# Rotary embedding of a fused attention and FFN kernel: the unturned first pair, and the rotation added in place in the feature tile

## The reference, cut to what matters

```python
def _rope(x, theta):
    T = x.shape[2]
    freqs = theta / 220.0 * _freqs_base()       # 8 frequencies, the first is 0
    ang = jnp.arange(T, dtype=jnp.float32)[:, None] * freqs
    cos, sin = (jnp.cos(ang), jnp.sin(ang))
    xr = x.reshape(*x.shape[:-1], HD // 2, 2)
    a, b = (xr[..., 0], xr[..., 1])
    rot = jnp.stack([a * cos - b * sin, a * sin + b * cos], axis=-1)
    return rot.reshape(x.shape).astype(x.dtype)
...
q = _rope(q, theta)
k = _rope(k, theta)
qk = jnp.einsum('bhkd,bhqd->bhkq', q, k) * scale
attn = _taylor_softmax(qk)          # (1 + x + x*x/2) / its sum
```

## Time and profile before

| | |
|---|---|
| median of 3 runs | 638.67 us (637.12 to 638.91) |
| the profiled execution, its own time | 640.14 us |
| its span, first to last instruction | 638.3 us |
| granted TensorE clock, mean over the span | 0.985 |
| busy: PE, DVE, ACT, POOL | 610.6, 585.2, 534.3, 445.5 us |

### The profile page before, as it was taken

The page is one execution under the profiler, slowest core; times in us unless marked ns, Lnnn a source line. Parts: engine busy times, 40 slices in busy tenths (PEclk is TensorE's granted clock), DMA queues, the critical chain, the costliest instruction groups (busy, mean ns, idle before and its releaser), DMA issues. The chain is left out here.

```text
span 638.3 us, 22975 instructions
## 1 busy us (share of the span) xinstructions
PE 610.6 (96%) x7592; PEld 472.3 (74%) x7592; DVE 585.2 (92%) x1489; ACT 534.3 (84%) x1504; POOL 445.5 (70%) x785
## 2 busy tenths in 40 slices
PE   8899999999999999999999999999999999999975
PEld 7776767676877778777787777678777776878764
DVE  5999999899999999999999989989989999986894
ACT  4267888898898989889898988889888988999972
POOL 2565456777777878787678967777886868764563
PEclk9999999999999999999999999999999999999985
DMA  7101131313232323322233142223232222130211
GB/s 249 34 3 41 24 75 26 76 33 110 45 104 53 97 70 78 89 71 72 51 76 86 46 126 66 69 51 114 52 105 56 76 54 79 30 85 20 68 36 42
DMA packets 55955, 43.67 MB, mean 68 GB/s; under 512 B 7200, under 2 KB 55712, under 8 KB 55840
## 3 DMA queue, kind: packets, MB, share of 16 engines
q1 hardware_dynamic: 55024, 41.42, 24.5%
q10 hardware_dynamic: 816, 0.79, 0.4%
HBM read 18.65 MB, written 8.39 MB: 42 GB/s over the span
## 5 line engine op out<-in xcount | busy, mean ns | idle before, releaser
L1200 ACT ACTIVATE feat<-ps_f 128x512 f32<-128x512 f32 x256 | 147.8, 604 | 9.1 <-PE ps_f L869 7.6
L688 DVE TENSOR_TENSOR kf<-kf 128x896 f32<-128x896 f32 (+1 forms) x128 | 128.8, 1012 | 1.0
L869 PE MATMUL ps_f<-qT,selr 128*128 128x512 f32 x320 | 120.8, 428 | 2.2 <-ACT feat L1200 1.4
L1042 PE MATMUL ps_mt<-kf,vp 128*32 128x153 f32 x2048 | 79.8, 296 | 2.0 <-ACT rm L1229 0.9
L1042 PEld LDWEIGHTS ps_mt<-kf,vp 128*32 128x32 f32 x2048 | 60.1, 109 | 17.9 <-issue 13.8
L1786 POOL TENSOR_TENSOR kf<-kf 128x128 f32<-128x128 f32 x64 | 42.9, 670 | 35.6 <-DVE kf L1550 35.4
L869 PEld LDWEIGHTS ps_f<-qT,selr 128*128 128x128 f32 x320 | 55.2, 189 | 12.3 <-ACT feat L1200 5.3
L688 POOL TENSOR_TENSOR kf<-kf 128x224 f32<-128x224 f32 x64 | 60.1, 939 | 2.2 <-DVE kf L1557 1.9
L1799 POOL TENSOR_TENSOR ve_y<-var_y,epst 128x1 f32<-128x1 f32 x64 | 24.9, 389 | 49.7 <-ACT squares_y L1312 49.2
L1774 POOL TENSOR_TENSOR qsp<-kf,qsp 128x256 fp32r<-128x256 f32 x64 | 54.5, 851 | 2.9 <-ACT qsp L1301 2.9
L1793 POOL TENSOR_TENSOR attT_l<-att,attT_h 128x256 fp32r<-128x256 f32 x56 | 43.4, 776 | 16.0 <-ACT attT_h L1241 15.6
(11 more groups left out here) (205 smaller groups left out, 1994.1 us busy)
## 6 DMA issues: line engine op xcount, KB each, us to landing
xc<-L_attn_x SPq DMA_DIRECT2D x16, 512.0 KB, 4.1
result<-fin SPq DMA_DIRECT2D x64, 128.0 KB, 3.0
xa<-L_attn_x SPq DMA_DIRECT2D x15, 512.0 KB, 3.9
heads_out<-osb SPq DMA_DIRECT2D x224, 32.0 KB, 2.0
shares<-sums SPq DMA_DIRECT2D x112, 64.0 KB
sums<-osb SPq DMA_DIRECT2D x224, 2.0 KB
wkqv<-L_attn_w_kv ACTq DMA_DIRECT2D x2, 256.0 KB, 4.4
xa<-L_attn_x SPq DMA_DIRECT2D x1, 384.0 KB, 5.7
```

What stands on the lines that cost most here:

```text
L688: return eng.tensor_tensor(dims(row, F_MAIN, [[FW, heads], [HD, NR - 1], [1, HD]]), dims(row, F_LIN, [[FW, heads], [0, NR - 1], [1, HD]]), ...
L869: pe.matmul(ps_f[i % 2][:, :], selr[:, i], queries, start=True, stop=True).then_inc(sel_done, 1)
L1042: mm = pe.matmul(ps_mt[qd // 2][VW * h:VW * (h + 1), (qd % 2) * NF:(qd % 2 + 1) * NF], vp[:, s2, qd * HQ + h], kf[:, s2, qd * HQ + h, 0:NF ...
L1200: act.activation(feat[:, p2, i], ps_f[i % 2][:, :], ACT.Square).then_inc(squared, 1)
```

## The change

Three things change together.

1. The rotation leaves the first pair of each head alone: `rope_sin` computes 14 of 16 features of each of the 32 heads (16 of the queries, 16 of the keys), 448 columns where it had 512, into the new tile `turned`; the sources start two words further.
2. `rope_cos` writes all 512 columns straight into the key and query fields of `kf`, and `rope_add` adds `turned` to 448 of them there, in place. With that the waits for the free buffer (`qlo_ready` and `sums_done` of the tile two before) move from `rope_add` to `rope_cos`; `rope_cos` no longer waits for the addition of the tile before. The tiles `t1` and `t2` are gone.
3. `ORDER` is another plan for all five queues, of the same lengths, and `IDLE` has 16 entries where it had 15.

```diff
+            def rotated(t, first):
+                return dims(kf[:, t.two, 0, 0:1], F_LIN + first, [[F_Q - F_LIN, 2], [FW, H], [1, HD - first]])
+
             def rope_cos(t):
-                cos = dims(cosT[:], t.tile * HD, [[0, 2 * H], [1, HD]])
+                cos = dims(cosT[:], t.tile * HD, [[0, 2], [0, H], [1, HD]])
                 if t.n == 1:
                     dve.wait_ge(tables_done, 1)
-                wait(dve, rope_ready, t.n - 1)
+                wait(dve, qlo_ready, t.n - 2)
+                wait(dve, sums_done, t.n - 2)
                 dve.wait_ge(qk_done, t.n)
-                dve.tensor_tensor(t1[:].rearrange("p (h d) -> p h d", d=HD), ps_qk[:, :].rearrange("p (h d) -> p h d", d=HD),
-                                  cos, ALU.mult).then_inc(qk_read, 1)
+                dve.tensor_tensor(rotated(t, 0), ps_qk[:, :].rearrange("p (a h d) -> p a h d", a=2, d=HD), cos, ALU.mult).then_inc(qk_read, 1)
 
             def rope_sin(t):
-                sin = dims(sinT[:], t.tile * HD, [[0, 2 * H], [2, 8], [1, 2]])
+                sin = dims(sinT[:], t.tile * HD + 2, [[0, 2 * H], [2, NR - 1], [1, 2]])
                 if t.n == 1:
                     dve.wait_ge(tables_done, 1)
                 wait(dve, rope_ready, t.n - 1)
                 dve.wait_ge(qk_done, t.n)
-                dve.tensor_tensor(dims(t2[:], 0, [[HD, 2 * H], [2, 8], [1, 2]]), dims(ps_qk[:, :], 1, [[HD, 2 * H], [2, 8], [-1, 2]]),
-                                  sin, ALU.mult).then_inc(qk_read, 1)
+                dve.tensor_tensor(dims(turned[:], 0, [[HD - 2, 2 * H], [2, NR - 1], [1, 2]]),
+                                  dims(ps_qk[:, :], 3, [[HD, 2 * H], [2, NR - 1], [-1, 2]]), sin, ALU.mult).then_inc(qk_read, 1)
 
             def rope_add(t):
                 dve.wait_ge(qk_read, 2 * t.n)
-                wait(dve, qlo_ready, t.n - 2)
-                wait(dve, sums_done, t.n - 2)
-                dve.tensor_tensor(dims(kf[:, t.two, 0, 0:1], F_LIN, [[F_Q - F_LIN, 2], [FW, H], [1, HD]]),
-                                  t1[:].rearrange("p (a h d) -> p a h d", a=2, d=HD),
-                                  t2[:].rearrange("p (a h d) -> p a h d", a=2, d=HD), ALU.add).then_inc(rope_ready, 1)
+                dve.tensor_tensor(rotated(t, 2), rotated(t, 2), turned[:], ALU.add).then_inc(rope_ready, 1)
...
-IDLE = {"fill": (1, 1, 1, 1, 1, 1, 4, 7, 10, 11, 14, 14, 14, 18, 23,), "drain": ()}
+IDLE = {"fill": (1, 1, 1, 1, 1, 1, 4, 7, 9, 9, 9, 9, 13, 18, 20, 28,), "drain": ()}
```

More of the change, by code:

```diff
@@ L180 @@
-        "sum_bias": ((3,), (), ()),
-        "sum_wo": ((4,), (), ()),
+        "centre_bias": ((102,), (), ()),
+        "copy_ffn_weight": ((94,), (), ()),
+        "copy_main": ((33, 83, 141, 209, 278,), (-2,), (494, 562, 636, 707, 779, 853, 921, 990, 1060,)),
+        "copy_q": ((23, 29, 38, 49, 59, 62, 71, 84, 101, 113, 125, 143, 162, 181, 200, 215, 231, 246, 263, 281, 300,
+            317, 334, 352, 372, 387, 405, 423, 440, 457, 476, 493, 512, 528, 547, 566, 582, 600, 617, 635, 654, 670,
+            687, 705, 723, 741, 758, 777, 795, 812, 829, 848, 867, 884, 901, 919, 935, 953, 971, 988, 1006, 1023, 1039,
+            1054,), (), ()),
@@ new lines @@
+        "high_kq": ((5,), (), ()),
+        "high_q": ((14, 17, 24, 30, 42, 50, 60, 67, 78, 91, 103, 114, 126, 145, 163, 183, 201, 217, 233, 251, 268, 288,
+            305, 323, 339, 359, 377, 394, 411, 433, 448, 465, 481, 503, 517, 534, 552, 575, 588, 607, 626, 646, 660,
+            680, 695, 715, 735, 749, 768, 794, 804, 820, 837, 859, 874, 890, 906, 927, 945, 961, 981, 1001, 1020,
+            1036,), (), ()),
+        "high_v": ((9,), (), ()),
+        "sines": ((4,), (), ()),
+        "split_ffn_weight": ((98,), (), ()),
@@ new lines @@
+        "low_ffn_weight": ((137,), (), ()),
+        "low_h": ((14, 18, 27, 39, 54, 65, 78, 86, 98, 106, 121, 136, 145, 156, 169, 198, 220, 240, 268, 286, 304, 324,
+            347, 368, 389, 407, 432, 455, 473, 491, 515, 535, 559, 580, 599, 621, 641, 661, 682, 706, 724, 744, 764,
+            789, 808, 829, 850, 872, 897, 915, 938, 958, 979, 1000, 1023, 1044, 1067, 1086, 1106, 1129, 1152, 1168,
+            1189, 1206,), (), ()),
+        "low_kq": ((6,), (), ()),
+        "low_v": ((15,), (), ()),
@@ new lines @@
+        "normalise_x": ((9, 13, 17, 29, 38, 52, 59, 70, 82, 90, 103, 119, 123, 143, 152, 164, 191, 204, 230, 254, 270,
[11 rows of a table added]
+        "rest_terms": ((64, 112, 175, 251, 330,), (-12,), (586, 666, 751, 837, 925, 1011, 1093, 1186, 1260,)),
+        "rope_add": ((22, 30, 40, 49, 62, 80, 88, 97, 108, 124, 140, 149, 158, 176, 199, 209, 237, 260, 278, 299, 321,
+            342, 364, 384, 404, 427, 452, 469, 488, 512, 536, 553, 578, 598, 617, 640, 659, 683, 703, 725, 745, 769,
+            788, 811, 830, 853, 878, 894, 916, 940, 959, 980, 1001, 1025, 1045, 1066, 1085, 1108, 1130, 1150, 1167,
+            1195, 1212, 1227,), (), ()),
@@ new lines @@
+        "rope_cos": ((20, 25, 35, 47, 61, 79, 87, 96, 107, 122, 139, 148, 157, 172, 197, 208, 236, 258, 275, 293, 315,
+            336, 361, 379, 399, 422, 451, 462, 482, 509, 534, 547, 570, 594, 613, 632, 656, 680, 696, 720, 741, 763,
+            782, 807, 827, 851, 873, 890, 912, 935, 956, 978, 997, 1021, 1043, 1064, 1083, 1105, 1127, 1146, 1162, 1183,
+            1205, 1223,), (), ()),
+        "rope_sin": ((21, 28, 36, 46, 60, 77, 85, 95, 102, 120, 138, 147, 153, 165, 186, 207, 232, 256, 272, 292, 312,
+            333, 357, 374, 395, 417, 450, 461, 480, 502, 533, 545, 568, 589, 605, 631, 651, 670, 691, 713, 734, 755,
+            774, 797, 819, 841, 868, 880, 902, 926, 954, 967, 988, 1014, 1041, 1056, 1077, 1101, 1119, 1141, 1159, 1180,
+            1207, 1217,), (), ()),
```

413 lines of the change are left out of this document (194 added, 219 removed), and 108 rows, old and new, of the table ORDER.

## The result

| | before | after |
|---|---|---|
| median of the runs | 638.33 us (637.12 to 638.91, 4 runs) | 642.93 us (641.67 to 643.64, 4 runs) |
| ratio to before, 95% interval | | 1.0069 (1.0050 to 1.0087) |
| span of the profiled execution | 638.3 us | 641.8 us |

The account below looks back on a forecast made before the run. DVE was taken to set the pace in its fullest stretches, together with PE; 7.8 us saved x 0.62 = 4.8 us off the profiled 640.14 gives 635.3, the median 1.5 us lower, so 634 us, range 629.5 to 641.5.

Parts of the forecast that it names:

- The price of each instruction: DVE rotation: sine 616 ns, addition 613 (650 at most), cosine's new output 0 to 4 ns; 0.132 us saved a tile.
- The dear in-place addition: Rival, DVE addition: stays at 679 ns because of odd words, only the sine saves, 636.3 us; chance 0.09.
- The moved waits: DVE cosine waiting for sums: 1.65 and 4.5 us at tiles 12 and 14 in the old order, 0 in the new.
- The slower rival: The moved wait stalls DVE at the cosine of 8 tiles, giving 642.1 us; chance 0.15.
- the profile had to show above 5 for it: Sign before the cosine: idle released by PE under 1 us in total; above 5 us the slower rival is right.
- How much of it reaches the end: Middle: six full DVE stretches give all, seven others three tenths, so 0.62 of 7.8 us, 4.8 us.
- The prediction's own sign in the profile: DVE idle in the middle: about 30 us confirms 0.62, 27 with a shorter middle all arriving, 35 PE bound.
- PE is the bound: Rival, middle: the saving only lengthens DVE's idle time; 638.7 us, with the order's noise 637 to 640.5; chance 0.20.
- The new order and the idle products: All queues' place tables and two more idle PE matmuls in the fill: 0, with 3 us each way.
- My closing line: Likeliest error: the order, as a gap in fill or drain differing by some us, all DVE durations as forecast.

Follow-up runs that it names:

- new_512: The changed kernel (new order, in-place addition, moved waits) with all 512 columns again in sine and addition: 644.45 us, ratio 1.0097 to the kernel before.
- order_only: The kernel before (old rotation, old waits) with the new ORDER and IDLE: 645.41 us, ratio 1.0123.
- columns_only: The kernel before, old order, waits and tiles, with only sine and addition cut to 448 of 512 columns: 637.19 us, ratio 0.9990.
- half_columns: The kernel before, old order and waits, with sine and addition cut to 256 of 512 columns: 634.58 us, ratio 0.9930.
- mended: The changed rotation in the old order, with the cosine of tiles 12, 14 and 62 moved right ahead of its addition: 638.44 us, ratio 1.0007.
- lean_mended: mended with PE's waits left out where an earlier PE wait already implies them: 636.97 us, ratio 0.9974.
- lean_before: The kernel before with PE's waits left out where an earlier PE wait already implies them: 636.33 us, ratio 0.9972.
- dve_plus: The kernel before with one more DVE product of 128 columns ahead of the cosine in each tile: 646.22 us, ratio 1.0129.

## Why the prediction was wrong

**The price of each instruction**: right. 616 and 613 ns were forecast, 614 and 618 measured, the cosine's new output 1 ns. The dear in-place addition (rival, 0.09) did not come. The Trainium skill, page "Vector Engine (DVE) Microarchitecture Reference", paragraph on the SBUF access granule (it stands in the section on measured stream behaviour), would make pairs at odd words, on both sources, dearer by a quarter. The addition, where only the key half of `kf` begins at an odd word, shows no sign of that. In the new order it takes 692 ns in place (new_512) and 693 ns from contiguous tiles (order_only), both with 512 columns; with 448 columns it takes 618 ns in the kernel after and, from contiguous tiles in the old order, 612 ns in columns_only.

**The moved waits**: right. In the old order they stall DVE by 1.69 and 4.45 us (1.65 and 4.5 forecast) and, at a tile that I had not looked at, by 3.21; the new order avoids them. The slower rival (0.15) named this as the way to a loss, so its time of 642.1 is near the result by another mechanism: the idle time before the cosine is 0.7 us after, and the profile had to show above 5 for it.

**"How much of it reaches the end", 0.62**: the first step that failed. By columns_only it is 0.6 / 7.8 = 0.08, by half_columns 0.15, and in the new order 1.8 / 7.8 = 0.23. The first and the last can't be told from nothing, but neither interval reaches the 4.8 us of the forecast. The step read a stretch with DVE at 98% as one in which DVE sets the pace and gives all. A saving there gives something only if what comes next on DVE is ready sooner too, and DVE's idle time of 31.6 for 26.9 us in columns_only says that mostly it was not. The prediction's own sign in the profile, DVE's idle time in the middle, came out at 33.8 us in the kernel after: nearer to the 35 of "PE is the bound" than to the 30 of 0.62. The rival "PE is the bound" gave the right figure for the columns alone (638.7, no gain) for a reason that half fails: PE lighter by two matmuls a tile gives as small a share.

**"The new order and the idle products: 0, with 3 us each way"**: the second step that failed, and the larger one: 7.9 us with the old rotation (order_only), 6.2 for all of the change but the columns (new_512), 4.0 with the new one against mended. I had no row for it and put the mean of what I did not know at 0, with a bound of half its real size. My closing line had the order as the likeliest cause of an error, but with a gap in fill or drain; it lies in the middle, spread over it from about 170 us on.

Summed: columns -0.6 to -1.8, moved waits 0, order +4 to +8, which gives 640.5 to 645.7 from 638.3; measured 642.9.

What the order's cost consists of is only partly settled. PE's implied waits, taken out, return 2 to 3 us more of it than they do elsewhere (within wide intervals). The wait of DVE for the DMAs of `sums`, 4.0 to 6.4 us in the kernels with the new order as written, is the most visible difference, but the lag grows by under 1 us across its largest stall, and most of the lag is there before it; no run took the wait away. Exchanging the value projection with its neighbour does not mend it. Nor was the plan swapped queue by queue, so which queue's new order costs the time stays open.

## What to carry to other kernels

A saving on an engine that is busy 92% is worth a share that only a run can tell: here 0.1 to 0.2 on any single engine (half for DVE with PE made lighter as well, though hardly beyond noise), and 0.4 to 0.8 when work is added. If two or three engines are above 80% and all run written sequences, start from the low share, and ask what the next instruction on the shortened engine waits for.

A new order of all queues is a change of its own. Swap it alone first; here it cost more than the rest could have brought, and a hand edit of three places in the old order served the new waits as well. lean_mended, 636.97 us (0.9974), is the best version with the changed rotation, 6 us ahead of the kernel as changed, and level with lean_before (0.9972), so the change itself brings nothing.

Look at how far the kernel has come, not only at how busy it was: PE's busy time in the middle was equal to 0.2 us, and the last tiles started 4 us later. Take the starts of one stage, tile by tile. Instruction counts at a fixed time mix long and short ones: 96 of the 101 matmuls missing at 560 us were one burst of 32 and one of 64 that fell on the other side of the line.

## What the runs showed of the hardware that was not expected

- PE's semaphore waits have a price even when an earlier wait already implies them: 320 fewer of them brought 1.8 to 4.6 us by the ratios, 6 to 14 ns each on average. The smallest of the four gains is only just clear of nothing (0.9945 to 0.9998).
- A DVE product of 128 columns added to each tile is recorded at 382 ns in the mean, where the median is 284 and the longest 822 (dve_plus). Its group by shape:

```profile
L1535 DVE TENSOR_TENSOR spare<-small 128x128 f32<-128x128 f32 x64 | 24.5, 382 | 0.3 <-PE ps_qk L798 0.3
```

- The two large products on `kf`, untouched by the change, went from 1132 and 891 ns to 1113 and 917. With the old rotation in the new order they take 1109 and 900, so the order alone moves them by 1% to 2%; by what, the runs don't show. Between before and after it is 2% to 3%, as much as 18 to 24 columns.
